# Layer 1 of a batch beside the next batch's attention, with the channel rotations by DMA

## What is computed

```python
# layer 0: self-attention over the 4096 positions
f = Wq gn(x) + bq        # 32 x 4096
g = Wk gn(x) + bk        # 32 x 4096
h = Wv gn(x) + bv        # 256 x 4096
beta = softmax(f^T g, over the first position)
x = x + gamma * (h beta)
# layer 1: products of channel pairs
y = relu(bn(W1 gn(x) + b1))                        # 32 channels
packed = y[rows] * y[cols]                         # all 528 pairs of channels
x = x + relu(bn(W2 packed + b2))
```

## Time and profile before

| | us |
|---|---|
| median of 3 runs | 2545.13 |
| lowest and highest | 2543.74, 2546.59 |
| the profiled execution's own span, first to last instruction | 2539.4 |
| TensorE busy, share of the span | 2371.8, 93% |
| VectorE busy | 1956.3, 77% |
| ScalarE busy | 1751.0, 69% |
| GpSimd busy | 492.5, 19% |

### The profile page before, as it was taken

How to read it: one execution, slowest core, us unless ns; L and a number is a source line. 1 busy time by engine, 2 the same in 40 slices (tenths; PEclk the granted TensorE clock), 3 DMA queues, 4 the chain that set the end, 5 groups by cost and what they waited for, 6 DMA issues and landing times.

```text
span 2539.4 us, 52331 instructions
## 1 busy us (share of the span) xinstructions
PE 2371.8 (93%) x17098; PEld 1662.9 (65%) x17098; DVE 1956.3 (77%) x3421; ACT 1751.0 (69%) x2841; POOL 492.5 (19%) x810
## 2 busy tenths in 40 slices
PE   4999999988899999998899999999889999999977
PEld 3677777772467777775256777777525777777742
DVE  8877777758877777775887777786688677877677
ACT  4677777767657777776666777677665777777765
POOL 2211111105511111100541111110153111111025
PEclk9999999999999999998999999999899999999989
DMA  2000000000000000000100000000010000000001
GB/s 89 2 9 8 8 8 8 9 18 34 35 1 9 8 8 8 8 18 9 42 27 1 9 8 8 11 14 10 14 45 19 1 0 0 0 0 0 2 12 55
DMA packets 18836, 36.66 MB, mean 14 GB/s; under 512 B 1296, under 2 KB 2192, under 8 KB 18704
## 3 DMA queue, kind: packets, MB, share of 16 engines
q1 hardware_dynamic: 18704, 34.99, 4.0%
HBM read 18.21 MB, written 16.78 MB: 14 GB/s over the span
## 4 chain that ended last, share of the span: by engine, by line
issue 72%; PE 9%; POOL 8%; DVE 8%; ACT 2%; POOLq 1%; DMA 0%; DVEq 0%; SPq 0%; ACTq 0%
POOL r L709 2%; PE acc L992 2%; DVE ph L521 2%; PE sps L963 2%; POOL r L712 2%; PE acc L963 2%; DVE htl L515 2%; DVE htl L529 1%; POOL mrow L710 1%; POOL r L711 1%; PE tps L998 1%; POOLq L194 1%; PE sps L1170 1%; PE sps L1166 1%; POOL xl L694 1%
## 5 line engine op out<-in xcount | busy, mean ns | idle before, releaser
L836 ACT ACTIVATE ph<-sps,esc 128x512 f16<-128x512 f32 x1024 | 704.0, 688 | 388.5 <-PE sps L1004 378.4
L1048 PE MATMUL acc<-hth,ph 128*128 128x257 f16 x4096 | 959.8, 274 | 1.0 <-ACT ot L827 0.9
L1049 PE MATMUL acc<-htl,ph 128*128 128x256 f16 x4096 | 958.4, 273 | 0.0
L450 DVE TENSOR_REDUCE mx<-tps 128x512 f32 (+1 forms) x1024 | 701.0, 688 | 290.8 <-PE tps L998 287.1
L491 DVE TENSOR_TENSOR pl<-p,ph 128x512 f16<-128x512 f32 x1024 | 699.5, 684 | 104.5 <-ACT p L837 104.5
L837 ACT ACTIVATE p<-sps,esc 128x512 f32<-128x512 f32 x1024 | 697.6, 681 | 0.0
L1058 PE MATMUL acc<-hth,pl 128*128 128x257 f16 x4096 | 621.5, 274 | 1.9
L1058 PEld LDWEIGHTS acc<-hth,pl 128*128 128x128 f16 x4096 | 397.7, 98 | 154.3 <-DVE pl L491 9.6
L1049 PEld LDWEIGHTS acc<-htl,ph 128*128 128x128 f16 x4096 | 401.8, 98 | 134.6 <-issue 1.3
L1048 PEld LDWEIGHTS acc<-hth,ph 128*128 128x128 f16 x4096 | 401.8, 98 | 80.2 <-ACT ot L827 21.4
L998 PE MATMUL tps<-fst,gst 96*128 96x512 f16 x1024 | 388.3, 384 | 11.0 <-DVE mx L450 6.1
(11 more groups left out here) (209 smaller groups left out, 1949.6 us busy)
## 6 DMA issues: line engine op xcount, KB each, us to landing
xa<-x SPq DMA_DIRECT2D x32, 512.0 KB, 3.6
out<-og SPq DMA_DIRECT2D x32, 512.0 KB, 2.7
og<-w SPq DMA_DIRECT2D x1, 608.0 KB, 4.4
p<-wv SPq DMA_DIRECT2D x1, 256.0 KB, 3.2
w1n<-w SPq DMA_DIRECT2D x1, 128.0 KB, 2.9
wqn<-wq SPq DMA_DIRECT2D x1, 96.0 KB, 2.1
wkn<-wk SPq DMA_DIRECT2D x1, 96.0 KB, 2.1
selh<-sel SPq DMA_DIRECT2D x1, 76.0 KB, 4.6
```

The costliest lines, as they stand in the source:

```text
L450: V.reduce_max(mx[:, ds(tile, 1), c], tps[par][:], AX).then_inc(t_free, 1)
L836: A(ph[:, u % SLOTS], sps[u % 2][:], ACT.Exp, scale=esc[:]).then_inc(ph_ok, 1)
L1048: mm(acc[j][:, 0:C + 1], w, hth[:, t], start=(t == 0), stop=False)
L1049: mm(acc[j][:, 0:C], w, htl[:, t], start=False, stop=False)
```

## The change

The three stages of a batch are taken apart. Layer 1 of batch b - 1 no longer runs by itself: its chunk J runs inside attention chunk J of batch b, spread over the 32 steps (`t` in the code). The last batch's layer 1 has no attention beside it and runs at the end. All loops are unrolled in the program. In detail:

- Queries and keys are one group of 6 matmuls with 128 rows of output (`queries_keys`). Six DMAs per chunk (`spread`) bring their rows to their places in `fst` and `gst`.
- The rotations are 19 DMAs per chunk (`rotate`), each of 32 partitions x 2 KB from `yb` to `rt`, in place of the five `select` matmuls. SyncE issues them. Beside attention GpSimd makes the products from them, in the last batch's layer 1 VectorE does.
- x is held in two buffers by batch parity; a separate load (`pass_through`) brings each chunk of the next batch for its statistics. Normalized chunks live in a ring of 4; those of the next batch's first four chunks are made in the last attention chunk.
- In attention the pieces use one PSUM bank (`tps[0]`), and `tps[1]` serves transposes, `project_y`, the row maxima and the W2 products of layer 1, one half of the output channels after the other.
- The row maxima of a chunk are split into parts once (128 x 4) and not four times (128 x 1).

The core of the diff, in the order SyncE, VectorE, GpSimd, ScalarE, TensorE (for the last four: attention first, then the last batch's layer 1, where shown; indentation is reduced by 8, and empty lines are left out):

```diff
+    def spread(b, c):
+        n, par, at = b * NCH + c, c % 2, slice(c * CH, (c + 1) * CH)
+        sp.wait_ge(qk_hi, n + 1)
+        sp.dma_start(fst[0:32, at], qkh[0:32, par]).then_inc(fg_in[par], 16)
+        sp.dma_start(fst[32:64, at], qkh[64:96, par]).then_inc(fg_in[par], 16)
+        sp.dma_start(gst[0:32, at], qkh[32:64, par]).then_inc(fg_in[par], 16)
+        sp.dma_start(gst[64:96, at], qkh[96:128, par]).then_inc(fg_in[par], 16)
+        sp.wait_ge(qk_lo, n + 1)
+        sp.dma_start(fst[64:96, at], qkl[64:96, par]).then_inc(fg_in[par], 16)
+        sp.dma_start(gst[32:64, at], qkl[32:64, par]).then_inc(fg_in[par], 16)
+    def rotate(n):
+        k = set_of(n)
+        sp.wait_ge(y_ok, n + 1)
+        if before(n) is not None:
+            sp.wait_ge(ql_ok, 5 * (before(n) + 1))
+        for e in range(TURNS):
+            sp.dma_start(rt[k][32 * (e % 4):32 * (e % 4) + 32, e // 4], yb[k][e:e + 32, :]).then_inc(rot_in[k], 16)
+        for r in range(3):
+            sp.dma_start(rt[k][32 * r:32 * r + 32, 4], yb[k][TURNS:TURNS + 32, :]).then_inc(rot_in[k], 16)
+    def store(b, c):
+        n = b * NCH + c
+        sp.wait_ge(res_ok, n + 1)
+        sp.dma_start(ov[b, :, :, c * CH:(c + 1) * CH], zt[set_of(n)]).then_inc(og_free[set_of(n)], 16)
...
+    for b in range(B):
         for c in range(NCH):
+            spread(b, c)
+            if c == 3 and b >= 2:
+                store(b - 2, NCH - 1)
+                load(b, NCH - 1)
+        for J in range(NCH):
+            if b and J:
+                store(b - 1, J - 1)
+                if b < LASTB:
+                    load(b + 1, J - 1)
+            if b < LASTB and J < NCH - 1:
+                pass_through(b + 1, J)
+            if b:
+                rotate((b - 1) * NCH + J)
+            if b < LASTB and J == NCH - 2:
+                pass_through(b + 1, NCH - 1)
+    store(LASTB - 1, NCH - 1)
+    rotate(SHARED)
     for c in range(NCH):
+        if c + 1 < NCH:
+            rotate(SHARED + c + 1)
+        store(LASTB, c)
...
+    def attend(b):
+        low_part(b * STEPS)
+        for J in range(NCH):
+            for t in range(NT):
+                u = b * STEPS + J * NT + t
+                slot, k = divmod(t, 8)
+                if t or J:
+                    k0 = (J * NT + t - 1) // 8 + LEAD
+                    if k0 < NT:
+                        piece_max(k0, (t - 1) % 8, 0)
+                if t == 24 and J + 1 < NCH:
+                    tile_max(b, J + 1)
+                if t == 0 and J:
+                    divide(b, J - 1)
+                if u + 1 < (b + 1) * STEPS:
+                    low_part(u + 1)
+                if t == 1 and b:
+                    second_normed(b - 1, J)
+                if J and t in (4, 6):
+                    finish(b, J - 1, (t - 4) // 2, 1)
+                if J and t in (5, 7):
+                    second_stats(b, J - 1, (t - 5) // 2, 1)
+                if b < LASTB and t in (12, 13) and J < NCH - 1:
+                    next_stats(b + 1, J, t - 12)
+                if b < LASTB and t in (26, 27) and J == NCH - 2:
+                    next_stats(b + 1, NCH - 1, t - 26)
+                    if t == 27:
+                        dve.wait_ge(xt_free, (b + 1) * NCH)
+                if b and 17 <= t <= 21:
+                    product_low((b - 1) * NCH + J, t - 17)
+                if b < LASTB and J == NCH - 1:
+                    if t == 8:
+                        next_moments(b)
+                    if t == 11:
+                        variance(0)
+                    if t == 14:
+                        bias(first_norm(b + 1), 0)
+                        dve.wait_ge(gn_ok, first_norm(b + 1) + 1)
+                    if 22 <= t < 22 + 2 * RING and t % 2 == 0:
+                        first_normed(b + 1, (t - 22) // 2)
...
+    for c in range(2):
+        second_normed(LASTB, c)
+    for grp in range(5):
+        product(SHARED, grp)
+    for c in range(NCH):
+        n = SHARED + c
+        if c + 2 < NCH:
+            second_normed(LASTB, c + 2)
+        for grp in range(5):
+            product_low(n, grp)
+            if c + 1 < NCH:
+                product(n + 1, grp)
...
+        for J in range(NCH):
+            if b:
+                second_low(b - 1, J)
+                if J:
+                    residual(b - 1, J - 1)
+            value_bias(b, J)
+            if b < LASTB and J == NCH - 1:
+                power(first_norm(b + 1), 0)
+            if b:
+                for grp in range(5):
+                    product((b - 1) * NCH + J, grp)
+            if J + 1 < NCH:
+                split_max(b * NCH + J + 1)
...
+    def attend(b):
+        for J in range(NCH):
+            for t in range(NT):
+                powers(b * STEPS + J * NT + t)
+                n = (b - 1) * NCH + J
+                if J and t == 1:
+                    divide(b, J - 1)
+                if b and J and t == 2:
+                    z_out(n - 1, 1, tps[1])
+                if b and t == 3:
+                    second_high(b - 1, J)
+                if b and t == 11:
+                    y_out(n, tps[1])
+                if b and 16 <= t <= 20:
+                    product_high(n, t - 16, None)
+                if b and t == 24:
+                    z_out(n, 0, tps[1])
+                if J + 1 < NCH and t == 28:
+                    row_copy(b, J + 1, tps[1])
+                if b < LASTB and J == NCH - 1 and 22 <= t < 22 + 2 * RING and t % 2 == 0:
+                    first_high(b + 1, (t - 22) // 2)
...
+    z_out(SHARED - 1, 1, tps[1])
+    for c in range(2):
+        second_high(LASTB, c)
+    y_out(SHARED, tps[0])
+    second_high(LASTB, 2)
+    for grp in range(5):
+        product_high(SHARED, grp, grp + 1)
+    for c in range(NCH):
+        n = SHARED + c
+        if c + 1 < NCH:
+            y_out(n + 1, tps[(c + 1) % 2])
+        if c + 3 < NCH:
+            second_high(LASTB, c + 3)
+        if c:
             for h in range(H2):
+                z_out(n - 1, h, acc[2 * ((c - 1) % 2) + h])
+        if c + 1 < NCH:
+            for grp in range(5):
+                product_high(n + 1, grp, 5 * (c + 1) + grp + 1)
...
+                if b and J and t == 0:
+                    for grp in (2, 3, 4):
+                        pairs(n - 1, 1, grp, tps[1])
+                if J and t in (3, 5):
+                    if b and t == 3:
+                        pe.wait_ge(z_ok, 2 * n)
+                    transposed(b, J - 1, (t - 3) // 2, 1)
...
+                if b and t in (8, 9):
+                    if t == 8:
+                        pe.wait_ge(xl_ok, second_job(b - 1, J) + 1)
+                        free(1)
+                    project_y(n, 0, tps[1], t - 8)
+                if b and 18 <= t <= 22:
+                    if t == 18:
+                        pe.wait_ge(y_ok, n + 1)
+                    pairs(n, 0, t - 18, tps[1])
+                if J + 1 < NCH and t == 26:
+                    if b:
+                        pe.wait_ge(z_ok, 2 * n + 1)
+                    else:
+                        free(1)
+                    rows(b, J + 1, tps[1])
+                if b and t in (29, 30):
+                    if t == 29:
+                        if J + 1 < NCH:
+                            pe.wait_ge(m_ok, b * NCH + J + 2)
+                        else:
+                            pe.wait_ge(z_ok, 2 * n + 1)
+                    pairs(n, 1, t - 29, tps[1])
+                if b < LASTB and J == NCH - 1 and t == 9:
+                    moments(first_norm(b + 1), 0)
...
+    for c in range(2):
+        pe.wait_ge(xl_ok, second_job(LASTB, c) + 1)
+        for i in range(H2):
+            project_y(SHARED + c, slot_of(LASTB, c), tps[c % 2], i)
+    for c in range(NCH):
+        n = SHARED + c
+        if c >= 2:
+            pe.wait_ge(z_ok, 2 * (n - 1))
+        for grp in range(5):
+            for h in range(H2):
+                pairs(n, h, grp, acc[2 * (c % 2) + h])
+        if c + 2 < NCH:
+            pe.wait_ge(xl_ok, second_job(LASTB, c + 2) + 1)
+            pe.wait_ge(y_ok, n + 1)
+            for i in range(H2):
+                project_y(n + 2, slot_of(LASTB, c + 2), tps[c % 2], i)
```

More of the change, by code:

```diff
@@ L327, in moments @@
[L327 to L336 removed]
+            over_stats(V.reciprocal(col(K_T), col(K_A)))
@@ new lines, in _, with normed @@
+            mark["weights"] = s.n
+            variance(0)
+            bias(0, 0)
+            dve.wait_ge(gn_ok, 1)
+            def normed(job, layer, src, at):
+                if job >= 2:
+                    dve.wait_ge(xl_ok, job - 1)
+                for h in range(H2):
+                    last = V.tensor_scalar(xn[:, job % 2, h], src[:, h, at], rstd[layer][:, h:h + 1],
+                                           nbias[layer][:, h:h + 1], ALU.mult, ALU.add)
+                last.then_inc(xn_ok, 1)
@@ L928, in _ @@
+            for h in range(H2):
+                z_out(SHARED + NCH - 1, h, acc[2 * ((NCH - 1) % 2) + h])
         @block.tensor
```

(10 more changed lines are left out.)

1277 lines of the change are left out of this document (527 added, 750 removed), and 6 rows, old and new, of tables (PARTS, PIECES).

## The result

The changed kernel takes 2734.72 us (median of 4 runs, 2733.97 to 2740.91), the kernel before 2544.43 (4 runs, 2542.88 to 2546.59): ratio 1.0753, 95% interval 1.0737 to 1.0769. It is slower, by 190 us. The forecast was slower, 2656 us, with a range of 2515 to 2765; the time lies in the range and 79 us above the forecast.

The account below looks back on a forecast made before the run. TensorE was taken to bound attention, with three 160 us gaps and a 108 us tail around it. Terms -297 + 169 + 72 + 24 + 12 + 131 = +111 gave span 2650, median 2656 us, range 2515 to 2765.

Parts of the forecast that it names:

- step 3: Attention: TensorE waits in each chunk for the 19 rotation DMAs, priced at 0.46 us an issue: +72 us.
- Step 2: Layer 1's matmuls move into attention, where TensorE is full: 24 chunks x 32 matmuls at 0.22 us, +169 us.
- Step 4: Attention: VectorE is delayed beside GpSimd's larger load, 1 us per chunk reaching TensorE: +24 us, at most +96.
- step 5: ScalarE normalizes the next batch's four chunks in a batch's last attention chunk: +12 us for three batches (0 to 18).
- Step 1: The three gaps between batches' attentions shrink to the projection, from 160.1 to 61 us each: -297 us.
- Case (d): Rival: issues back up at 0.65 us each, +82 us in attention and +27 in the tail: 2765 us; 12%.
- Step 6: Last batch's layer 1, after attention, gets a longer chain with turns of 29 us: 239 us for 108, +131.
- case (e): Rival: TensorE keeps full clock in the tail, 24 us a turn and 12 off the end: 2614 us; 8%.
- (a): Rival: a 32-row issue costs about 0.1 us, so attention's stalls go and the tail loses 52: 2532 us; 13%.
- (b): Rival: the tail's chain is also as short as before and nothing stalls: 2429 us; 5%.
- (c): Rival: the lock between VectorE and GpSimd in attention costs its upper bound, 96 us: 2728 us; 10%.
- sign of 549 us: Expected in the profile after: attention of 549 us (69 a chunk) from the second batch on.

Follow-up runs that it names:

- Five copies: Changed kernel with each chunk's 19 rotation DMAs replaced by 5 copies of 128 rows, about the same bytes, rotation left out: 2487.5 us.
- run out of HBM: Changed kernel with the 19 rotation DMAs reading the same rows and bytes from x in HBM instead of yb: 2639.9 us.
- Experiment 12: Changed kernel with four of GpSimd's five products in attention cut to one column and 22 unused matmuls put in TensorE's stall: 2697.1 us.
- experiments 6 and 7: Changed kernel with layer 1's scales computed later, 2731.6 us; then also issues split with GpSimd, consumers two steps later, tail rotation before store, 2491.4 us.
- combined kernel: Changed kernel with GpSimd issuing 9 of 19 rotation DMAs, layer 1 two steps later in attention, tail rotation before store, scales later: 2491.4 us.
- stall filled: Changed kernel with 22 unused 512-column matmuls at the end of step 16 of each attention chunk of the last three batches: 2728.2 us.

## Why the prediction was right in sign and 79 us short

The time fell into the range because errors of both signs met, 83 us in all against the forecast span of 2650: step 3 came out 115 us too low, and steps 2, 4 and 5 together were 33 us too high for batches 1 to 3 and 6 for batch 0, the tail 5 and the gaps 2; the start, which the sum left out, added 14. By its own steps:

**Step 1, the gaps.** 62.2, 62.6 and 62.2 us; 61 was taken, and 160.1 for each gap before, of which the second and third were 163.2 and 163.0. Right, with two small errors that cancel.

**Step 2, the matmuls.** Five copies shows attention with the rotation's stall gone: +167.9 us for 24 chunks against 169. Right in the main, though not to the microsecond. TensorE stands still for 33.6 us of these three attentions and for 14.4 of before's, so some 19 us of the 167.9 are waits (for VectorE's additions to x, 14.1, and its maxima, 11.8, above all). In return TensorE's other work became shorter: in batch 0's attention, beside which no layer 1 runs, it is busy for 451.1 us in the changed kernel and for 456.8 in the one before. Steps 4 and 5, +24 for three batches and +12, find room for no more than these 19 us: as long as TensorE doesn't stop for the rotation, most of VectorE's delays are absorbed. They are there (VectorE's subtraction went from 684 to 739 ns on average), they lie off the path. Of step 5's 4 us in batch 0, TensorE's waits in the last chunk show 2.

**Step 3, the stall, is where it failed.** +72 was forecast, and 355.3 - 167.9 = 187.4 us were measured. The chain was the forecast one, link by link: relu to 880.10, landing and wait for it 2.1 us after the last issue's start (1.9 taken), product 1.3 (1.4), high part and exponentials 1.8 (1.95), and TensorE ran 12.3 us on its own, from 879.28 to 891.57, as worked out. One term of it was mis-sized and one was missing.
- The price of an issue: 0.63 us for 0.46. The run out of HBM, at 0.46, has 73.4 us less attention. The price of the earlier trace rows was for another kind of DMA, and the text took it though it noted that no row showed one from SBUF to SBUF. It was right that rows and bytes don't matter. Case (d), 0.65, had 12%; by the measured price it was nearly the case. With 0.63 the prediction's own working gives a wait of 145 us in place of 72; TensorE's was 149.1 - 7.8 = 141.3. The Trainium skill, DMA: Bandwidth & Descriptors, section Anatomy of one DMA, which the prediction set against its price, describes DMAs that GpSimd issues; these were SyncE's.
- A term that wasn't there: what a stall costs beyond its own length. At 0.46 us TensorE's wait was 79.4 - 7.8 = 71.6 us (24 waits of 2.1 to 3.6), close to the forecast's 72, but attention was 114.0 us longer than with five copies. The other 42.4 us are the restart, 1.8 us a chunk; at the changed kernel's price they are 187.4 - 141.3 = 46.1, 1.9 a chunk. Experiment 12 takes 1.7 a chunk away again by removing two causes, half clock and VectorE's slower operations beside GpSimd. Batch 2's attention by busy time (columns as in the earlier trace rows), with five copies and with the rotation out of HBM, and the HBM run's first slow matmul behind the stall that ends at 888.71:

```profile
1218.90:1736.50 517.60, 506.09 (x3879) 377.36 (x3879) 400.67 (x651) 381.58 (x621) 147.11 (x130) 1.00 0.12 43
1256.50:1812.00 555.50, 520.73 (x3879) 382.47 (x3879) 402.72 (x651) 380.98 (x621) 139.03 (x130) 0.97 0.13 39
```
```profile
890.49 0.61 PE L1051 MATMUL tps<-fst,gst 96*128 96x512 f16 x1 [0.51 <-DVE mx L535]
```

The same 3879 matmuls keep TensorE busy for 14.6 us longer, at a granted clock of 0.97 instead of 1.00; over the three batches it is 40.3 of the 114.0 us, and the other 73.7 are standing still. So half clock is in the HBM run's restart too. (That the second cause of experiment 12 is at work there as well is inferred.)

The sum is then 167.9 + 71.6 + 42.4 + 73.4 = 355.3. It comes out by construction, since each term is the difference of two runs; what it shows is the shares.

**Step 4 once more.** The Trainium skill, SBUF — State Buffer, section SBUF: two separate sides, calls the port pair of VectorE and GpSimd an exclusive lock. The trace agrees: operations with two SBUF inputs take 1.14 to 1.75 us beside GpSimd's products and 0.68 without them. What I had wrong is its place: it costs little through the chunk (see step 2) and counts most where VectorE restarts behind a stall.

**Step 6, the tail.** 239 us was forecast, 234.0 measured, by errors that cancel: luck, in this part. One turn of the changed kernel, store to store:

```profile
2645.63 0.38 SPq L289 DMA_DIRECT2D out<-htl  x1
2646.11 10.14 SPq L282 DMA_DIRECT2D htl<-htl  x16
...
2656.28 1.86 SPq L284 DMA_DIRECT2D htl<-htl  x3
...
2659.57 0.69 DVE L588 TENSOR_TENSOR htl<-htl 128x512 f32<-128x512 f32 x1 [21.74 <-DMA htl<-htl]
...
2668.36 0.78 ACT L890 ACTIVATE yb<-tps,t1a,s1a 128x512 f32<-128x512 f32 x1 [2.39 <-PE tps L1079]
...
2669.88 2.48 POOL L771 TENSOR_TENSOR zt<-zt,xb 128x512 f32<-128x512 f32 x2 [0.93 <-ACT zt L907]
...
2672.39 0.38 SPq L289 DMA_DIRECT2D out<-zt  x1
```
```profile
2659.50:2665.20 5.70, 4.28 (x11) 1.57 (x12) 5.57 (x9) 2.52 (x4) 0.00 (x0) 0.51 0.01 1
2665.20:2672.80 7.60, 4.84 (x23) 1.98 (x21) 1.62 (x4) 2.75 (x4) 5.06 (x4) 1.00 0.01 2
```

The turn is 26.76 us (29 forecast). Its issues take 12.0 us (18 x 0.46 = 8.3 forecast), but from landing to relu it is 8.8 us, not 12: the second pair of rows has TensorE at a granted clock of 0.51 (the level of 1.2 GHz) only for the first 5.7 us, in which VectorE is busy for 5.57 and sets the pace anyway, and at 1.00 (2.4 GHz) for all that follows. The forecast had priced the pairs and `project_y` at half clock throughout. It had also strung two normalizations, both outputs and the addition behind the relu, 5.7 us to the store; the trace has 3.3 (2669.14 to 2672.39), with the addition starting between the two outputs and no normalization ahead of them. That is also what speaks against case (e) as stated: the full clock comes back by itself after 5.7 us, and with VectorE the bound of these 5.7 us it could save little there. At 0.46 us an issue the tail is 211.5, 27 below the forecast, which is the size of these errors together with those of the tail's start and end; the price puts 22.5 on it.

**Not in the sum: the start.** +14.1 us to the first exponential. In the changed kernel's trace VectorE has the first batch's `nbias` at 41.42 (38.38 before), ScalarE waits 6.3 us for the scales ahead of its first q and k copy, and 7.7 us for the spreading DMAs of the joint q and k group. How much each is worth isn't settled; experiments 6 and 7 put 2 to 8 us on the scales. The working looked at the gaps between batches and not at the one projection that hides nothing.

**The rivals.** (a) and (b) needed an issue of 0.1 us and are out; both issue rows exclude it. Five copies, at 2487 us, shows the change with a cheap rotation: faster than before, between the 2532 of (a) and the 2429 of (b). The sum changes its sign at an issue of 0.19 us by its own terms, not at 0.15. (c) reached 2728, close to the measured time, but by a mechanism that is worth 8.4 us by itself (four of the five products left out), and with five copies, where GpSimd did all its work beside VectorE, its 96 us find no room. (d) is the nearest in cause. Of (e) it came true that the full clock is there for a part of each turn; the tail was 234, not its 197.

The sign of 549 us for the later attentions left out step 5 (554 for the first two of them); measured were 577 to 583.

"Without the tail the sum is -20" was wrong as well: the tail and the issues share the cost. Without the tail's 126.1 the change would still be 68 us slower.

## What to carry to other kernels

When work moves under a saturated engine, count the DMAs it brings, not their bytes, and take the price of an issue from a row with the same source and destination; a queue of 19 is a serial chain of 12 us that no bandwidth figure shows. Price a stall at its length plus the restart, and expect several limits to lie side by side there, so that removing one shows nothing. A chain that costs more than its cover could be mended here (2734.7 to 2491.4 us) by splitting the issue over two queues, by putting its consumer later, and by issuing it ahead of a store.

## What the runs showed of the hardware

- Issued one behind the other by SyncE, a DMA from SBUF to SBUF cost 0.63 us with 32 rows (64 KB) and 0.62 to 0.65 with 128 (256 KB); one of 32 rows out of HBM cost 0.46, and eight of 512 KB out of HBM 0.65 each. What sets the price isn't known from these runs.
- GpSimd issued the same DMA in 0.50 us. Beside it SyncE kept nearly its pace (10 in 6.2 to 7.0 us in the combined kernel's tail; 11 in 6.9 to 8.2 in attention, 0.69 from one to the next on average, against 0.66 alone), but slowed down to 0.85 each (10 in 8.5 to 9.1) where its part also stood right behind a store of 512 KB.
- After 5.1 to 6.6 us of standing still in the middle of attention TensorE's scores took 0.61 us instead of 0.39 (0.50 in one of 24 chunks); with work in the gap (stall filled) they took 0.61 in two chunks only. After waits of 2.1 to 3.6 us (rotation out of HBM) they took 0.61 in 8 of 24 chunks; in 13 of the other 16 the granted clock fell to half within the next 8 us.
- VectorE's operations with two SBUF inputs took up to 1.75 us beside GpSimd's products, 0.68 without; the maxima, with one PSUM input, took 0.68 in both.
